# Attention weights laid out on the host, and the first transfers cut in panels

## The chip, the cores and the metric

The kernel runs on one NeuronCore of a Trainium2 chip. The metric is the device time of one execution in microseconds (us). A core has five engines with queues of their own, which are kept in step by semaphores only: TensorE (PE, with its weight loads as PEld), VectorE (DVE), ScalarE (ACT), GpSimd (POOL) and SyncE (SP), which here issues transfers only. ACT issues a few transfers too. SBUF is the working memory with 128 partitions, PSUM holds eight banks that matmuls write. `ps` is PSUM in the profile's names.

## What is computed

Four residual layers over x (8 sequences of 256 tokens, 128 features): attention A with a table of relative biases, a routed feed-forward net of 8 experts, causal attention B with a low-rank key/value, and the same feed-forward net again.

```python
x = L0_attn_a_x                                        # (8, 256, 128)
x = x + attn_a(layernorm(x), w_qkv, w_out, rel_bias)
x = x + ffn(layernorm(x), Wr, br, ln_g, ln_b, W1, b1, W2, b2)
x = x + attn_b(layernorm(x), w_kv_down, w_kv_up, w_q, w_out)
x = x + ffn(layernorm(x), ...)

def attn_a(x, w_qkv, w_out, rel_bias):                 # 16 heads of 64
    qkv = (x @ w_qkv.T).reshape(b, t, 64, 3, 16).transpose(3, 0, 4, 1, 2)
    q, k, v = qkv                                      # w_qkv: (3072, 128)
    scores = q @ k.T / 8 + rel_bias[j - i + t - 1]
    out = softmax(scores) @ v
    return merge_heads(out) @ w_out.T                  # w_out: (128, 1024)
```

Attention B has the weights `w_q` (128 x 1024), `w_kv_down` (128 x 128), `w_kv_up` (128 x 2048) and `w_out_b` (1024 x 128).

## The kernel before

The work is written out by hand in steps. A step `s` from 0 to 63 is one unit, `u`: two heads of one sequence, so there are `NU` = 64 units in an attention, eight to a sequence. Steps beyond 63 are the 25 tiles of the feed-forward net; then the same steps run again with `st` = 1 for attention B and the second net. Each engine runs its own list of these steps in order, so the order on an engine is that of its functions `begin` and `step`.

A unit goes this way. PE computes queries and keys of the unit into bank `PT_` (`QK(u)`, six matmuls of 256 columns in two groups of three: every product is split in a high and a low part, and `three` adds high*high, low*high and high*low). ACT copies them to `qk` (`T(u)`); only then may PE write `PT_` again. PE computes the scores (`S(u)`, 16 matmuls), for two units in a row on odd steps. DVE subtracts them from the bias table `T` and takes the minimum (`S(u)`, L1365). ACT takes the exponentials (L1046), DVE the reciprocal of their sums (L1378), POOL multiplies (L429), PE transposes (`TR`), DVE and ACT copy a half each from PSUM (`pt`, L1393 and L1034), PE multiplies by the values (`PV`, L742).

The high and low parts of the weights are made on the core. ACT writes the high part (`act_high`, L971) with a conversion to the narrower type, DVE the low part, the rest (`low`, L1232 and L1234). For attention A the weights come in as they are stored, with the features of x along the row, so the contraction is not on the partitions: `wqn`, `wkn`, `wvn` and `won` are loaded, PE transposes them into PSUM (`pe_weights`, `value_weights`, `extra`), and ACT and DVE read them from there. `w_part` n = 0 and 1 are queries and keys of units 0 to 3, n = 2 and 3 of units 4 to 7, n odd the keys.

The start, before step 0 ends, runs like this. SP issues in this order the first 128 KB of x (`x[:, 0:2]`), four transfers of halves of `wqn` and `wkn`, a half of `wvn`, the bias table for units 0 and 1 (`T[0:4]`, 512 KB), more of x, `T[4:8]`, `won`, `T[8:16]` and the rest of x. ACT issues the other halves (64 partitions each) of the same weights. DVE takes the statistics of x (`pre_a`), POOL the power, DVE normalises (`pre_a2`, tile `xh`), PE transposes (`pre_b`), ACT and DVE split it in `xth` and `xtl`. DVE then makes the low parts of panels 0 to 2, the bias table of units 0 and 1 (`biases(0)`, L1344 and L1345) and both low parts of the value weights, before its `S(0)`. POOL makes the tables of the other units.

The weights of attention B come during the first feed-forward net, on SP, once the 64th unit is done (L1785 to L1795): twelve transfers with rows of 64 or 128 elements for the order by unit. Behind them in SP's queue stand `results`, which write tiles of the net back.

Of the kernel before, what the change touches and what calls it, by code (L numbers as in the profile page):

```python
# [179 lines left out]
def build(nc, t):  # L180
# [148 lines left out]
    wq3 = t["w_qkv"].rearrange("(d c f h k) x -> c h d f k x", c=3, f=4, h=2, k=2)  # L329

    def heads(j, hh, a, b):

        return wq3[j, hh, :, a:b, :, :]

    def of_heads(w, a):

        return w[:, a:a + 1024].rearrange("p (f h k d) -> p h f k d", f=4, h=2, k=2)
# [268 lines left out]
    def pe_steps(st):  # L606
# [206 lines left out]
        def extra(s):  # L813
            for g in range(2 if s == 4 else 0):
                if g == 0:
                    pe.wait_ge(d_won, 16)
# [1039 lines left out]
```

## Time and profile before

| | us |
|---|---|
| median of 3 runs | 650.25 (649.43 to 650.32) |
| the profiled execution | 648.84 |
| its span, first to last instruction | 647.6 |
| PE busy | 625.2 (97%) |
| DVE busy | 511.1 (79%) |
| ACT busy | 524.6 (81%) |
| POOL busy | 354.9 (55%) |

The profile is of one execution. 1.2 us of its time lie outside the span. The busy time of PE contains the modelled ends of pipelined matmuls, so it is read beside the idle times in front of instructions. The chain of waits, followed back from the last instruction, tells what set the end.

### The profile page before, as it was taken

How to read it: one execution, taken by the hardware profiler on the slowest of the kernel's cores; microseconds unless marked ns; L12 is line 12 of the kernel's file. 1: busy time of each engine (PE TensorE's matmuls, PEld its weight loads, DVE VectorE, ACT ScalarE, POOL GpSimd, SP SyncE). 2: the span in 40 equal slices, each digit the busy share in tenths (PEclk: the TensorE clock that was granted, in tenths of full speed). 3: DMA queues.
4: the chain of work that ended last, by engine and by line, in shares of the span. 5: the costliest groups of instructions: out<-in, count | busy, mean ns of one | idle time of the engine just before them, and what ended most of it. 6: DMA issues, size and time to landing. Idle time of an engine off the chain costs nothing.

```text
span 647.6 us, 22119 instructions
## 1 busy us (share of the span) xinstructions
PE 625.2 (97%) x7454; PEld 537.3 (83%) x7454; DVE 511.1 (79%) x2211; ACT 524.6 (81%) x1776; POOL 354.9 (55%) x674
## 2 busy tenths in 40 slices
PE   5999999999999999999999899999999999999997
PEld 4678787877878788879988789888888988888997
DVE  4986878778887888888865787887988799898833
ACT  3898888889788878785675998998989898986664
POOL 5653645455475557643206554555757665772746
PEclk9999999999999999999999999999999999999999
DMA  8999989999991000133531100000000000113140
GB/s 263 317 307 308 289 211 319 313 310 311 282 287 41 3 2 27 43 100 83 166 107 37 40 3 3 8 2 6 7 7 21 16 4 2 36 49 93 55 129 18
DMA packets 90319, 74.78 MB, mean 115 GB/s; under 512 B 12225, under 2 KB 87111, under 8 KB 90080
## 3 DMA queue, kind: packets, MB, share of 16 engines
q1 hardware_dynamic: 86512, 66.24, 36.6%
q0 software_dynamic: 2848, 6.33, 3.0%
q8 instruction: 62, 1.02, 0.6%
q10 hardware_dynamic: 848, 0.79, 0.4%
q14 instruction: 49, 0.40, 0.2%
HBM read 19.93 MB, written 54.00 MB: 114 GB/s over the span
## 4 chain that ended last, share of the span: by engine, by line
PE 79%; DVE 7%; issue 4%; POOL 3%; ACT 3%; DMA 3%; SPq 1%; DVEq 0%; POOLq 0%; ACTq 0%
PE ps L578 16%; PE ps L694 13%; PE ps L742 13%; PE ps L573 10%; PE ps L575 8%; PE ps L574 8%; PE ps L848 5%; PE ps L864 4%; DVE ring L1365 2%; ACT ring L1046 2%; DMA T<-in_bias 1%; POOL out L449 1%; POOL ring L429 1%; PE ps L780 1%; DVE v L1330 1%
## 5 line engine op out<-in xcount | busy, mean ns | idle before, releaser
L429 POOL TENSOR_SCALAR ring<-ring,rs 128x256 f32<-128x256 f32 (+1 forms) x500 | 217.1, 451 | 129.4 <-DVE rs L1378 127.5
L1046 ACT ACTIVATE ring<-ring,mn 128x256 f32<-128x256 f32 (+1 forms) x512 | 243.7, 483 | 1.5 <-DVE mn L1365 1.4
L578 PE MATMUL ps<-ident,ring 128*128 128x128 f32 x896 | 122.0, 275 | 3.6 <-DVE ol L1337 1.8
L578 PEld LDWEIGHTS ps<-ident,ring 128*128 128x128 f32 x896 | 101.9, 142 | 12.5 <-issue 4.1
L694 PE MATMUL ps<-qk 64*64 64x256 f32 (+3 forms) x2048 | 107.1, 344 | 1.3 <-ACT qk L1018 0.8
L742 PE MATMUL ps<-pt,v 64*64 64x256 f32 (+3 forms) x2048 | 102.9, 338 | 2.0 <-ACT pt L1034 1.5
L1046 ACT ACTIVATION_READ_ACCUMULATOR ring<-ring,mn 128x1 f32 x512 | 101.7, 199 | 0.0
L742 PEld LDWEIGHTS ps<-pt,v 64*64 64x64 f32 x2048 | 76.5, 133 | 26.1 <-ACT pt L1034 6.6
L1393 DVE COPY pt<-ps 128x512 f32<-128x512 f32 (+1 forms) x128 | 75.5, 589 | 20.3 <-PE ps L578 18.8
L694 PEld LDWEIGHTS ps<-qk 64*64 64x64 f32 x2048 | 65.0, 133 | 28.4 <-issue 12.3
L1018 ACT COPY qk<-ps 128x512 f32<-128x512 f32 x128 | 74.3, 580 | 12.4 <-PE ps L575 12.2
L1365 DVE CUSTOM_DVE_ANT_0 ring<-ps,cm 128x128 f32<-128x128 f32 (+1 forms) x256 | 73.5, 352 | 0.9 <-PE ps L694 0.3
L1034 ACT COPY pt<-ps 128x512 f32<-128x512 f32 (+1 forms) x128 | 64.2, 502 | 2.0 <-PE ps L578 1.6
L1012 ACT ACTIVATE oh<-ps 128x256 fp32r<-128x256 f32 x128 | 41.9, 380 | 29.4 <-PE ps L742 29.1
L573 PE MATMUL ps<-xth,wqkh 128*128 128x256 f32 x192 | 65.2, 339 | 0.0
L1095 ACT ACTIVATE f_ht<-ps,f_w 128x128 f32<-128x128 f32 x136 | 38.4, 377 | 22.6 <-PE ps L848 22.6
L1365 DVE CUSTOM_DVE_ANT_0 ring<-ps,T 128x256 f32<-128x256 f32 x136 | 55.9, 420 | 0.0
L1365 DVE CUSTOM_DVE_ANT_1 ring<-ps,T 128x256 f32<-128x256 f32 x120 | 50.3, 419 | 5.4 <-PE ps L694 4.5
L574 PE MATMUL ps<-xth,wqkl 128*128 128x256 f32 x192 | 54.2, 282 | 0.0
L575 PE MATMUL ps<-xtl,wqkh 128*128 128x256 f32 x192 | 54.2, 282 | 0.0
L1330 DVE COPY v<-ps 64x512 f32<-64x512 f32 x64 | 44.0, 688 | 12.9 <-PE ps L575 11.0
L864 PE MATMUL ps<-w,f_ht 128*128 (+1 forms) x400 | 52.4, 277 | 0.5 <-ACT f_ht L1095 0.4
(210 smaller groups left out, 1297.3 us busy)
## 6 DMA issues: line engine op xcount, KB each, us to landing
xs_scratch<-f_ys SPq DMA_DIRECT2D x16, 2064.0 KB, 21.5
yr_scratch<-f_ys SPq DMA_DIRECT2D x8, 1024.0 KB
f_xs<-xs_scratch SPq DMA_DIRECT2D x50, 129.0 KB, 2.3
w<-in_W SPq DMA_DIRECT2D x16, 256.0 KB, 6.0
xs_scratch<-f_ys SPq DMA_DIRECT2D x2, 1677.0 KB, 20.5
yr_scratch<-f_ys SPq DMA_DIRECT2D x25, 64.0 KB, 1.8
T<-in_bias SPq DMA_DIRECT2D x2, 512.0 KB, 8.2
T<-in_bias SPq DMA_DIRECT2D x1, 1024.0 KB, 10.7
```

Of the source, the lines that this page charges most:

```text
L429: i = pool.tensor_scalar(part, part, rs[:, q], 1.0, ALU.mult, ALU.mult)
L573: pe.matmul(out, ah, bh, start=first, stop=False)
L574: pe.matmul(out, al, bh, start=False, stop=False)
L575: return pe.matmul(out, ah, bl, start=False, stop=last)
L578: return pe.transpose(out, src, ident if order is None else order)
L694: i = pe.matmul(PS[u % 2][hh][cols, 256 * it:256 * it + w], qk[rows, 64 * n:64 * n + 64], qk[rows, 256:256 + w], start=True, stop=True)
L742: i = pe.matmul(PO[hh][64 * k:64 * k + 64, lo:256], a_v[b % 2][rows, q, 64 * (c + k):64 * (c + k) + 64], a_pt[(U0 + u + k) % 2][rows, half ...
L864: i = pe.matmul(y_bank(n)[:, 0:128], f_ht[n % 3][:, 128 * f:128 * f + 128], w2[:, bass.ds(e * 4 + f, 1), :].rearrange("p a n -> p (a n)"), ...
L1018: act.copy(a_qk[(U0 + u) % 2][:, :], PT_[:, :]).then_inc(a_t, 1)
L1046: i = act.activation(part, part, ACT.Exp, bias=mn[:, q], scale=-1.0, accum_out=sm[:, q])
L1365: i = dve.tensor_tensor_reduce(scores(ring, hh, it, w), by_64(bank[:, 256 * it:256 * it + w]), table(st, head_of(c, hh), it), 1.0, BIG, AL ...
L1393: dve.tensor_copy(pt[:, 1, r], PP[1][:, r]).then_inc(v_pt1, 1)
```

## The change

1. The host (numpy) lays out `w_qkv`, `w_out_a`, `w_q`, `w_kv_up` and `w_out_b` so that the contraction is on the partitions and the columns stand in the order of the units.
2. No weight is transposed on PE. `pe_weights`, `value_weights` and `extra` are gone from PE; ACT and DVE read the raw weights in SBUF and wait for the transfer instead of for PE. `wvh` and `wvl` are written in halves of 512 contiguous columns.
3. Queries and keys come in three panels instead of two: units 0 and 1, 2 and 3, 4 to 7. So there are six parts (`products(0)` to `products(5)`), four of 256 columns and two of 512.
4. Transfers at the start: ACT issues panel 0, panel 2 and the two halves of the value weights, over all 128 partitions; SP issues x, panel 1, then the table. The third table transfer is cut in two, with `won` between.
5. ACT runs parts 0 to 3 before `xth`, parts 4 and 5 after it and before `T(0)`, and the two halves of the value weights on steps 1 and 2 instead of both on step 1. DVE runs parts 0 and 1 between the statistics and the normalisation, 2 and 3 behind it, the second value half and parts 4 and 5 on step 2.
6. For attention B four transfers stand where twelve stood.

```diff
+PANELS = [(0, 2), (2, 4), (4, 8)]
...
+    raws = at_first(pre, *(sb(n, [128, 1024], scope=pre) for n in ("wqkn0", "wvn0", "wqkn1", "wvn1")))
...
             if b == 0:
-                pe.wait_ge(a_wv, 3 if st else 2)
-                pe.wait_ge(v_wv, 3 if st else 2)
+                pe.wait_ge(a_wv, 3 if st else half_ + 1)
+                pe.wait_ge(v_wv, 3 if st else half_ + 1)
...
-            if st == 0 and u in (0, 4):
-                pe.wait_ge(a_m, 2 + u // 2)
-                pe.wait_ge(v_m, 2 + u // 2)
+            for g, (first, _) in enumerate(PANELS):
+                if st == 0 and u == first:
+                    pe.wait_ge(a_m, 2 * g + 2)
+                    pe.wait_ge(v_m, 2 * g + 2)
...
             pre_b(0)
-            for n in range(4):
-                if n % 2 == 0:
-                    pe.wait_ge(d_wqk[n // 2], 64)
-                pe_weights(n)
...
         def products(*ns):
             for n in ns:
-                act.wait_ge(t_m, n + 1)
-                act_high(w_part(wqkh, n), m_bank(n)[:, :], a_m, scale=w_scale(n))
+                act.wait_ge(d_wqk[n // 2], 16)
+                act_high(w_part(wqkh, n), w_raw(n), a_m, scale=w_scale(n))
...
     def act_program():
+        for g in (0, 2):
+            act.dma_start(raw(g), t["w_qkv"][:, panel(g)]).then_inc(d_wqk[g], 16)
         for g in range(2):
-            for j, w in enumerate((wqn, wkn)):
-                act.dma_start(w[64:128, 4 * g:4 * g + 4, :], heads(j, 1, 2 * g, 2 * g + 2)).then_inc(d_wqk[g], 16)
-        act.dma_start(wvn[64:128, :, :], heads(2, 1, 0, 4)).then_inc(d_wv, 16)
+            act.dma_start(wvn[g][:, 0:512], t["w_qkv"][:, 2048 + 512 * g:2560 + 512 * g]).then_inc(d_wv[g], 16)
...
     def sp_program():
         sp.dma_start(x[:, 0:2, :], xv[:, 0:2, :]).then_inc(d_x[0], 16)
-        for g in range(2):
-            for j, w in enumerate((wqn, wkn)):
-                sp.dma_start(w[0:64, 4 * g:4 * g + 4, :], heads(j, 0, 2 * g, 2 * g + 2)).then_inc(d_wqk[g], 16)
-        sp.dma_start(wvn[0:64, :, :], heads(2, 0, 0, 4)).then_inc(d_wv, 16)
+        sp.dma_start(raw(1), t["w_qkv"][:, panel(1)]).then_inc(d_wqk[1], 16)
         sp.dma_start(a_T[:, 0:4, :], t["bias"][:, 0:4, :]).then_inc(d_T[0], 16)
         sp.dma_start(x[:, 2:4, :], xv[:, 2:4, :]).then_inc(d_x[1], 16)
         sp.dma_start(a_T[:, 4:8, :], t["bias"][:, 4:8, :]).then_inc(d_T[1], 16)
-        sp.dma_start(won[:, :], t["w_out_a"]).then_inc(d_won, 16)
-        sp.dma_start(a_T[:, 8:16, :], t["bias"][:, 8:16, :]).then_inc(d_T[2], 16)
+        sp.dma_start(a_T[:, 8:12, :], t["bias"][:, 8:12, :]).then_inc(d_T[2], 16)
+        sp.dma_start(won[:, :, :], t["w_out_a"]).then_inc(d_won, 16)
+        sp.dma_start(a_T[:, 12:16, :], t["bias"][:, 12:16, :]).then_inc(d_T[3], 16)
...
+        sp.dma_start(bq[:, :], t["w_q"]).then_inc(d_bq, 16)
+        sp.dma_start(bu[:, :], t["w_kv_up"]).then_inc(d_bu, 16)
         sp.dma_start(bkd, t["w_kv_down"]).then_inc(d_bkd, 16)
-        sp.dma_start(bo[:, :, :], t["w_out_b"].rearrange("(c p) n -> p c n", p=128)).then_inc(d_bo, 16)
+        sp.dma_start(bo[:, :, :], t["w_out_b"]).then_inc(d_bo, 16)
```

The order on DVE from the normalisation to the first scores. `wqkl` and `wvl` are low parts of weights, `cT` and `T` the bias table, `ISA ring,mn` is the first operation of `S(0)`. Before:

```order
L1252 TENSOR_SCALAR xh<-row,mv,rstd 128x128 [waits p_pow0]
L1252 TENSOR_SCALAR xh<-row,mv,rstd 128x128
L1232 TENSOR_TENSOR xtl<-ps,xth 128x256 [waits a_x]
L1234 SCALAR_TENSOR_TENSOR wqkl<-ps,wqkh 128x512 [waits a_m]
L1232 TENSOR_TENSOR wqkl<-ps,wqkh 128x512 [waits a_m]
L1234 SCALAR_TENSOR_TENSOR wqkl<-ps,wqkh 128x512 [waits a_m]
L1294 COPY run<-rows_e 128x8 [waits p_set]
L1344 COPY cT<-T 128x4 [waits d_T0,v_c]
L1345 TENSOR_TENSOR T<-cT,T 128x1024 [waits v_c]
L1232 TENSOR_TENSOR wvl<-ps,wvh 128x4x2x64 [waits a_wv,v_c]
L1232 TENSOR_TENSOR wvl<-ps,wvh 128x4x2x64 [waits a_wv]
L1365 ISA ring,mn<-ps,T 128x4x64 [waits t_s,p_set]
```

And of the change, on the same engine and at the same place:

```order
L1202 SCALAR_TENSOR_TENSOR wqkl<-wqkn,wqkh 128x256 [waits a_m]
L1200 TENSOR_TENSOR wqkl<-wqkn,wqkh 128x256 [waits a_m]
L1220 TENSOR_SCALAR xh<-row,mv,rstd 128x128 [waits p_pow0]
L1220 TENSOR_SCALAR xh<-row,mv,rstd 128x128
L1202 SCALAR_TENSOR_TENSOR wqkl<-wqkn,wqkh 128x256 [waits a_m]
L1200 TENSOR_TENSOR wqkl<-wqkn,wqkh 128x256 [waits a_m]
L1200 TENSOR_TENSOR xtl<-ps,xth 128x256 [waits a_x]
L1262 COPY run<-rows_e 128x8 [waits p_set]
L1312 COPY cT<-T 128x4 [waits d_T0,v_c]
L1313 TENSOR_TENSOR T<-cT,T 128x1024 [waits v_c]
L1200 TENSOR_TENSOR wvl<-wvn,wvh 128x512 [waits a_wv,v_c]
L1337 ISA ring,mn<-ps,T 128x4x64 [waits t_s,p_set]
```

Two low parts of 256 columns now stand ahead of the normalisation and two behind it; of the value weights one half is left ahead of `S(0)`.

DVE between the last operation of `S(1)` and `S(2)`. `COPY v` takes values from PSUM, `stats` to `rstd` are the statistics of sequence 1. Before:

```order
L1330 COPY v<-ps 64x512 [waits t_v]
L1232 TENSOR_TENSOR wqkl<-ps,wqkh 128x512 [waits a_m]
L1239 BN_STATS stats<-row 128x6 [waits d_x1]
L1242 BN_STATS stats<-row 128x6
L1243 BN_AGGR mv<-stats 128x2 [waits v_c]
L1244 BN_AGGR mv<-stats 128x2
L1248 TENSOR_SCALAR rstd<-mv 128x2 [waits v_c]
L1330 COPY v<-ps 64x512 [waits t_v]
L1378 RECIPROCAL rs<-sm 128x4 [waits a_ex]
```

And of the change:

```order
L1200 TENSOR_TENSOR wvl<-wvn,wvh 128x512 [waits a_wv]
L1202 SCALAR_TENSOR_TENSOR wqkl<-wqkn,wqkh 128x512 [waits a_m]
L1200 TENSOR_TENSOR wqkl<-wqkn,wqkh 128x512 [waits a_m]
L1298 COPY v<-ps 64x512 [waits t_v]
L1207 BN_STATS stats<-row 128x6 [waits d_x1]
L1210 BN_STATS stats<-row 128x6
L1211 BN_AGGR mv<-stats 128x2 [waits v_c]
L1212 BN_AGGR mv<-stats 128x2
L1216 TENSOR_SCALAR rstd<-mv 128x2 [waits v_c]
L1298 COPY v<-ps 64x512 [waits t_v]
L1350 RECIPROCAL rs<-sm 128x4 [waits a_ex]
```

Three operations of 512 columns stand where one stood.

The start of ACT's queue, up to `T(1)`, with the transfers that it issues. Before:

```order
L1209 DMA wqn<-in_w_qkv 64x2x256 [waits barrier_Pool_Activation_PE_DVE_SP_release]
L1209 DMA wkn<-in_w_qkv 64x2x256
L1209 DMA wqn<-in_w_qkv 64x2x256
L1209 DMA wkn<-in_w_qkv 64x2x256
L1210 DMA wvn<-in_w_qkv 64x4x256
L971 ACT_TABLE_LOAD
L971 ACTIVATE xth<-ps 128x256 [waits t_x]
L971 ACTIVATE wqkh<-ps 128x512 [waits t_m] x3
L1018 COPY qk<-ps 128x512 [waits t_t]
L971 ACTIVATE wvh<-ps 128x4x2x64 [waits t_wv] x2
L1018 COPY qk<-ps 128x512 [waits t_t]
```

And of the change:

```order
L1176 DMA wqkn<-in_w_qkv 128x512 [waits barrier_Pool_Activation_PE_DVE_SP_release]
L1176 DMA wqkn<-in_w_qkv 128x1024
L1178 DMA wvn<-in_w_qkv 128x512 x2
L930 ACT_TABLE_LOAD
L930 ACTIVATE wqkh<-wqkn 128x256 [waits d_wqk0] x2
L930 ACTIVATE wqkh<-wqkn 128x256 [waits d_wqk1] x2
L930 ACTIVATE xth<-ps 128x256 [waits t_x]
L930 ACTIVATE wqkh<-wqkn 128x512 [waits d_wqk2] x2
L989 COPY qk<-ps 128x512 [waits t_t]
L930 ACTIVATE wvh<-wvn 128x512 [waits d_wv0]
L989 COPY qk<-ps 128x512 [waits t_t]
```

Each group of weights now waits for its own transfer, and the two parts of panel 2 stand between `xth` and the first `COPY qk`, which is `T(0)`.

## Rows read from the trace of the kernel before

**Rows 1.** The page: the span, and the chain that ended last, by engine.

```profile
span 647.6 us, 22119 instructions
...
PE 79%; DVE 7%; issue 4%; POOL 3%; ACT 3%; DMA 3%; SPq 1%; DVEq 0%; POOLq 0%; ACTq 0%
```

**Rows 2.** Stretches: busy us of PE, PEld, DVE, ACT, POOL; granted clock; DMA share; GB/s.

```profile
8.00:9.00 1.00, 0.34 (x2) 0.00 (x0) 0.69 (x1) 0.72 (x2) 0.71 (x5) 1.00 1.13 232
...
14.00:15.00 1.00, 1.00 (x18) 0.63 (x21) 0.96 (x3) 0.94 (x3) 0.50 (x2) 1.00 1.07 438
...
60.00:290.00 230.00, 228.42 (x2736) 185.26 (x2734) 190.04 (x793) 193.58 (x630) 127.62 (x244) 1.00 0.66 183
```

**Rows 3.** The chain that ended last, 0 to 60 us: start, us, what.

```profile
4.71 7.90 DMA T<-in_bias
...
15.44 0.42 DVE ring L1365
...
27.67 0.61 DVE pt L1393
28.32 0.66 PE ps L578 x4
```

**Rows 4.** Timeline of PE: start, us, operation, count, idle before and its releaser.

```profile
9.22 1.11 PE L578 MATMUL ps<-ident,wqn 128*128 128x128 f32 x4 [0.87 <-DMA wkn<-in_w_qkv]
...
10.84 0.56 PE L573 MATMUL ps<-xth,wqkh 128*128 128x256 f32 x1
...
11.84 0.41 PE L574 MATMUL ps<-xth,wqkl 128*128 128x256 f32 x1
12.05 0.41 PE L575 MATMUL ps<-xtl,wqkh 128*128 128x256 f32 x1
12.26 1.26 PE L578 MATMUL ps<-ident,wvn 128*128 128x128 f32 x8
...
14.16 1.96 PE L694 MATMUL ps<-qk 64*64 64x256 f32 x32
...
16.27 0.28 PE L574 MATMUL ps<-xth,wqkl 128*128 128x256 f32 x1
16.39 0.28 PE L575 MATMUL ps<-xtl,wqkh 128*128 128x256 f32 x1
```

**Rows 5.** Timeline of DVE, 3 to 28 us.

```profile
3.35 0.29 DVE L1239 BATCH_NORM_STATS2 stats<-row 128x6 f32<-128x128 f32 x1 [3.35 <-DMA row<-in_x]
...
5.23 0.60 DVE L1252 TENSOR_SCALAR xh<-row,mv,rstd 128x128 f32<-128x128 f32 x2 [0.91 <-POOL rstd L395]
7.09 0.42 DVE L1232 TENSOR_TENSOR xtl<-ps,xth 128x256 fp32r<-128x256 f32 x1 [1.26 <-ACT xth L971]
...
14.17 1.29 DVE L1232 TENSOR_TENSOR wvl<-ps,wvh 128x512 fp32r<-128x512 f32 x2
...
19.04 0.69 DVE L1232 TENSOR_TENSOR wqkl<-ps,wqkh 128x512 fp32r<-128x512 f32 x1
19.64 0.28 DVE L1239 BATCH_NORM_STATS2 stats<-row 128x6 f32<-128x128 f32 x1
```

**Rows 6.** Timeline of ACT, 4 to 13 us.

```profile
4.35 1.28 ACT L971 ACT_TABLE_LOAD   x1 [4.35 <-issue]
6.67 0.38 ACT L971 ACTIVATE xth<-ps 128x256 fp32r<-128x256 f32 x1 [1.04 <-PE ps L578]
...
12.50 0.58 ACT L1018 COPY qk<-ps 128x512 f32<-128x512 f32 x1 [1.54 <-PE ps L575]
```

**Rows 7.** ACT's queue: start and us of the last transfer that it issues.

```profile
3.69 0.63 ACTq L1210 DMA_DIRECT2D wvn<-in_w_qkv  x1
```

**Rows 8.** SP's queue near 300 us, and a low part made from SBUF (tile `bq`).

```profile
299.96 2.90 SPq L1789 DMA_DIRECT2D bq<-in_w_q  x4
...
308.06 3.48 SPq L1753 DMA_DIRECT2D yr_scratch<-f_ys  x5
...
L1234 DVE SCALAR_TENSOR_TENSOR wqkl<-bq,wqkh x1: 1215/1215/1215, 323.3 to 323.3; 128x1024 fp32r<-128x1024 f32 x1
```

More of the change, by code:

```diff
@@ L328, in build, with panel, raw @@
     xv = t["x"].rearrange("b (s p) d -> p (b s) d", p=128)
[L329 to L337, printed above, removed]
+    def panel(g):
+        a, b = PANELS[g]
+        return slice(256 * a, 256 * b)
+    def raw(g):
+        a, b = PANELS[g]
+        return wqkn[a // 4][:, 256 * (a % 4):256 * (a % 4) + 256 * (b - a)]
     def load(engine, values, a, b, most):
@@ L811, in post_d @@
             pe.matmul(PX[:, n8:2 * n8], ones[:, :], h, start=True, stop=True).then_inc(t_cnt, 1)
[L813 to L816, printed above, removed]
-                bank = spare(("wo", g), v_wo, g + 1)
-                for j in range(4):
-                    i = tr(bank[:, 128 * j:128 * j + 128], won[:, 512 * g + 128 * j:512 * g + 128 * j + 128])
-                i.then_inc(t_wo, 1)
         def XT(g):
@@ L1125, in begin, with value_weights @@
         def begin():
+            products(0, 1, 2, 3)
             pre_b(0)
-            products(0, 1, 2)
-        def value_weights():
-            for g in range(2):
-                act.wait_ge(t_wv, g + 1)
-                act_high(by_parity(wvh[:, :])[:, 4 * g:4 * g + 4], by_unit(ps[4 + g][:, :]), a_wv)
+            products(4, 5)
+        def value_weights(g):
+            act.wait_ge(d_wv[g], 16)
+            act_high(halves(wvh, g), wvn[g][:, 0:512], a_wv)
         def step(s):
@@ L1352, in S @@
                 dve.wait_ge(p_set, k_T0)
+            if st == 0 and u in (1, 3):
+                dve.wait_ge(v_wv, (u + 1) // 2)
+            if st == 0 and u == 2:
+                dve.wait_ge(v_m, 2 * len(PANELS))
             if st == 0 and u in (2, 4, 6):
@@ L1571, in begin, with value_weights @@
             pre_a(0)
+            products(0, 1)
             pre_a2(0)
+            products(2, 3)
             pre_b(0)
-            products(0, 1, 2)
-        def value_weights():
-            for g in range(2):
-                low(by_parity(wvl[:, :])[:, 4 * g:4 * g + 4], by_unit(ps[4 + g][:, :]),
-                    by_parity(wvh[:, :])[:, 4 * g:4 * g + 4], a_wv, g + 1, v_wv)
+        def value_weights(g):
+            low(halves(wvl, g), wvn[g][:, 0:512], halves(wvh, g), a_wv, g + 1, v_wv)
         def step(s):
@@ L1586, in step @@
                 start_rows()
-            if st == 0 and s == 1:
-                value_weights()
+            if st == 0 and s in (1, 2):
+                value_weights(s - 1)
+            if st == 0 and s == 2:
+                products(4, 5)
             if s % 2 == 0 and 6 <= s < NU:
@@ L1831, with _by_units, _by_halves, _w_qkv @@
           "L0_ffn_ln_b": "ln_b", "L0_ffn_W1": "W1", "L0_ffn_b1": "b1", "L0_ffn_W2": "W2", "L0_ffn_b2": "b2"}
+def _by_units(a):
+    return a.reshape(128, 4, 2, 2, 64).transpose(0, 1, 3, 2, 4).reshape(128, 1024)
+def _by_halves(a):
+    return a.reshape(128, 4, 2, 2, 64).transpose(0, 2, 1, 3, 4).reshape(128, 1024)
+def _w_qkv(a):
+    q, k, v = a.reshape(64, 3, 1024 // 64, 128).transpose(1, 3, 2, 0).reshape(3, 128, 1024)
+    q, k = _by_units(q), _by_units(k)
+    panels = [w[:, 128 * a:128 * b] for a, b in PANELS for w in (q, k)]
+    return np.concatenate(panels + [_by_halves(v)], axis=1)
+_LAYOUT = {"w_qkv": _w_qkv,
+           "w_out_a": lambda a: a.reshape(128, 8, 128).transpose(2, 1, 0),
+           "w_q": _by_units,
+           "w_kv_up": lambda a: np.concatenate([_by_units(a[:, :1024]), _by_halves(a[:, 1024:])], axis=1),
+           "w_out_b": lambda a: a.reshape(8, 128, 128).transpose(1, 0, 2)}
 def kernel(**inputs):
```

90 lines of the change are left out of this document (33 added, 57 removed).

## The prediction

> **What bounds the kernel now.** I read the page first: a span of 647.6 us, of which PE holds 79% of the chain that ended last [rows 1]. In the table of stretches PE is busy for 228.42 of the 230 us from 60 to 290 [rows 2]. There a saving on any other engine is worth nothing, and the change takes no work from PE there. So the whole question is how early PE enters that steady flow. The chain read in order of time answers it [rows 3]: SP's issues, then the wait for the first bias table, which lands at 4.71 + 7.90 = 12.61 us, then DVE without a break (table, low parts of the value weights, S(0) at 15.44 and so on) to its copy `pt` at 27.67, and from 28.32 on PE. The reader is to see that the PE transposes of the weights are not on this path. What counts is the time at which DVE ends that `pt` copy. It ends at 27.67 + 0.61 = 28.28; I call that the hand-over. A gain there is carried through a PE-bound kernel to the end, one for one.
>
> **From S(0) to the hand-over, DVE's work grows.** DVE runs from 15.44 to 28.28 without idle time worth naming, 12.84 us. In this stretch the change drops one low part of 512 columns and adds three: the second half of the value weights and both parts of panel 2. One costs 0.60 us from PSUM (19.04 to the next start at 19.64 [rows 5]) and, from SBUF, 1215 ns for 1024 columns, so 0.61 for 512 [rows 8]. Net +1.22 us, giving 14.06. I take it in full, since DVE has no gap there to hide it. The bounds are 0 (if DVE would have waited at the next scores anyway) and 1.22. So the hand-over is S(0) + 14.06, and S(0) must start before 14.22 for a gain.
>
> **When S(0) can start.** Before, DVE reached it at 15.44, right behind the two `wvl` (14.17 + 1.29) [rows 5], while PE had begun S(0) at 14.16 [rows 4], 1.3 us ahead. The table was late, and the scores were nearly as late. I work out both chains of the change.
>
> *The table.* The transfers of both issuing engines share the engines that move them, so I count bytes, and take it that the two queues get equal shares. SP has 128 KB of x, 256 of panel 1 and 512 of table: 896 KB, and as much again goes to ACT's queue meanwhile, 1792 KB or 1835 thousand bytes. The first 128 KB of x were used at 3.35 [rows 5]; the rest is 1704 thousand bytes. The stretch from 8 to 9 us, with weight rows of 1 KB, moved 232 GB/s; that from 14 to 15, with table rows of 4 KB, 438 [rows 2]. The change has rows of 2 to 4 KB. So 7.3 or 3.9 us more: 10.7 or 7.2, and I take 9.0. Either beats 12.61. By the Trainium skill, "DMA: Bandwidth & Descriptors", section "Bandwidth", a 1 MB load runs at 341 GB/s; as an estimate that would put the table at 8.3. `cT`, table and low part of the first value half cost some 1.4 + 0.6 us, so DVE is free by 11.7 even where it waits for ACT's `wvh`. The table is no longer what holds S(0).
>
> *The scores.* (a) ACT's last issue began at 3.69 as the fifth [rows 7]; the change has four, so it is over near 3.6, and the 1.28 us table load [rows 6] ends near 4.9. (b) Panel 0 lands between 4.2 and 5.0 by the same byte count, so ACT makes part 0 at 4.9 to 5.3 (0.38 for 256 columns [rows 6]) and part 1 by 5.5. (c) DVE makes both low parts by 6.0 (0.42 each, overlapping). Before, the normalisation started at 5.23 [rows 5]; now it stands behind them and starts at 5.95: this is 0.7 us lost. (d) From the normalisation to the start of `xtl` took 7.09 - 5.23 = 1.86, so `xtl` is at 7.8 and done at 8.2; parts 2 and 3 fit into DVE's wait. Panel 1 (between 4.8 and 6.1) is in time for them. (e) QK(0) starts at 8.3 instead of 10.84 [rows 4]. From its first matmul to `T(0)` took 12.50 - 10.84 = 1.66 [rows 4, 6]. That puts `T(0)` at 9.95. (f) In front of `T(0)` ACT now waits for panel 2, behind 768 KB of its queue: 1442 thousand bytes after 3.35 take 3.3 to 6.2 us, landing 6.6 to 9.5. Two parts, each at the 0.58 that ACT takes for 512 columns [rows 6], then end at 7.8 to 10.7; I take 9.1, hidden by QK(0), and keep 0.7 us late as the bound. (g) `T(0)` ends at 10.55, QK(1) starts at 10.7. Before, the value transposes filled this place, 12.26 to 13.3 [rows 4]. (h) QK(1) takes 1.3 at 0.21 a matmul, to 12.0. (i) S(0) is half of 32 matmuls that took 1.89 to the next start, so 0.95; at half the rate 1.7 to 1.9.
>
> **The clock of PE.** The granted clock reads 1.00 in the stretches I show [rows 2], but the rows of PE say otherwise: 256 columns step by 0.21 us up to 12.05, which is the level of 1.2 GHz, and by 0.12 at 16.27, that of 2.4 GHz [rows 4]. It rose after PE had worked without a break from 9.22. In the change PE has a gap between QK(0) and QK(1), so it may rise later than 12. The Trainium skill, "TensorE: Matmul & The Clock Gate", "Part 1: The HAM clock gate (the "warmup" mystery)", says that the clock depends on how busy PE has recently been; by that rule the removal of the transposes, which kept PE busy, speaks against this change, and the later trace agrees in so far as the rate rose only after unbroken work; by it alone the time would be that of rival B. The prices are from rows: fast from 12.0, S(0) is done at 12.95 and starts on DVE at 13.0; rising inside S(0), 13.3; slow throughout, 13.75, and S(1) is then another 0.3 late for DVE.
>
> **The sum.** Hand-over at 13.3 + 14.06 = 27.36 against 28.28: 0.9 us earlier. Span 646.7, time 648.84 - 0.9 = 647.9 for an execution like the profiled one. This one lies 1.4 us below the median of 650.25, so I subtract the same 0.9 there: 649.35. ACT is nearly as full as DVE before the hand-over, but it loses one 512 part and is released by PE's `T(2)` even earlier than DVE; I cost it at nothing, and if that cover is gone it costs up to the 0.6 of one part. POOL's tables wait for landings only: the second comes before 14.3 and is needed with S(2) after 20; nothing.
>
> **The parts worth nothing.** The 32 transposes on PE (8 in 1.26 us [rows 4]) lie before the hand-over, where PE is not the bound. The eight of `won` also go, with the wait of the next `xh` transpose for `wo`; DVE sets that stretch, so nothing. The split of the third table transfer: the table of the last units is asked for after 20 us; nothing. Near 300 us SP issues twelve transfers from 299.96 and reaches its first result at 308.06 [rows 8]. Eight issues fewer are about 5 us for SP, but PE and its neighbours go on meanwhile, and `bq` is first split by DVE at 323.3 [rows 8]: hidden by the tiles, nothing. If a result tile were awaited it would be a gain, bounded by 5 us; no row shows such a wait.
>
> **Rivals.** *A, the lead is carried in full:* PE is at the fast level by 12, or DVE's added 1.22 us fall into waits. Hand-over 1.3 to 2.4 us early: 648.4. For it: the first value half and the table leave DVE idle before S(0). Against: rows 5 have no gap behind S(0). *B, nothing is left:* the clock rises late (13.75 + 14.06 + 0.3 = 28.1), or panel 2 lands at 9.5: 650.1, the gain all spent on DVE's added parts and PE's slow start. *C, slower:* ACT's queue gets much less than half of the bandwidth, since x, panel 1, both tables and `won` follow on SP without pause. `T(0)` stands behind panel 2; S(0) on DVE then passes 14.22 when the panel lands after about 9.7, and it is slower by over 1.3 us when it lands after 11.1. At 12 us: 652.5. Against: 786 thousand bytes from 3.35 to 12 would be 91 GB/s, below half of 232, the slower rate shown. *D, the change doesn't do what it says:* some later wait, such as PE's for the added values at step 3, takes the lead away; 650.25, part of B's chance.
>
> **How the numbers follow.** A measurement of this kernel can tell 0.2%, 1.3 us, from no change. The forecast (0.3 to 1.3 us faster) has 0.48, A 0.31, B with D 0.16, C 0.05. Predicted: 649.35. The range reaches over A and B to 647.9 and 650.6, leaving C and the far ends. Faster by over 0.2% has A's chance and a little of the forecast's edge, 0.33; slower has C and a crumb, 0.06; the rest, 0.61, is within 0.2%.
>
> **What would show it.** Right, step by step: the first table lands before 11; QK(0) starts near 8.3; `T(0)` is near 10 with no wait for panel 2; DVE waits for PE, not for a transfer, at S(0), near 13.3; three low parts stand between S(1) and S(2); DVE's `pt` copy ends near 27.4; the stretch from 60 to 290 us keeps 228 us of PE. Wrong: a chain that still holds a transfer after 10 us, S(0) after 14, or a difference that arises only after 60 us.

## The result, and the profile after

The change makes the kernel slower: 655.09 us median (654.20 to 655.45, 4 runs) against 650.23 before, a ratio of 1.0080 with a 95% interval of 1.0063 to 1.0097. The profiled execution took 654.2 us. Its page begins with the span, 5.2 us over that of before [rows 1]:

```profile
span 652.8 us, 22049 instructions
```

Two readings say where to search. The stretch from 60 to 290 us has not moved (228.42 us of PE before [rows 2]). And the fourth pair of scores behind the hand-over, the same work in both kernels, starts 5.21 us later. The table of stretches of after (columns as in rows 2), and the rows of PE's timeline, first of before and then of after:

```profile
60.00:290.00 230.00, 229.25 (x2736) 186.48 (x2729) 190.12 (x793) 193.95 (x630) 129.64 (x249) 1.00 0.60 174
```

```profile
52.02 1.96 PE L694 MATMUL ps<-qk 64*64 64x256 f32 x32
```

```profile
57.23 1.96 PE L677 MATMUL ps<-qk 64*64 64x256 f32 x32
```

So the whole loss lies ahead of 57 us. From here on I compare kernels at this pair of scores: whatever follows it takes 595.6 us in both profiles. The chain of after up to there, beside [rows 3]:

```profile
0.81 3.65 DMA row<-in_x
...
12.99 1.96 PE ps L677 x16
15.09 0.42 DVE ring L1337
...
17.93 1.90 DVE wvl L1200
...
28.28 2.99 DVE wo L1200 x2
31.27 0.61 DVE pt L1365
31.93 1.01 PE ps L570 x4
32.94 3.16 PE ps L677 x32
```

The table of biases has left the chain, as forecast, and S(0) starts on DVE at 15.09, even 0.35 before its old time. The loss comes behind it. The hand-over has moved from 28.28 to 31.88, and PE's first work behind it is slow. Two rows are far too long. DVE's timeline of after (beside [rows 5]):

```profile
4.48 0.29 DVE L1207 BATCH_NORM_STATS2 stats<-row 128x6 f32<-128x128 f32 x1 [4.48 <-DMA row<-in_x]
...
11.92 0.69 DVE L1200 TENSOR_TENSOR wvl<-wvn,wvh 128x512 fp32r<-128x512 f32 x1 [1.55 <-ACT wvh L930]
17.85 1.98 DVE L1200 TENSOR_TENSOR wvl<-wvn,wvh 128x512 fp32r<-128x512 f32 x1
...
28.28 2.99 DVE L1200 TENSOR_TENSOR wo<-won,wo 128x512 fp32r<-128x512 f32 x2
31.19 0.68 DVE L1365 COPY pt<-ps 128x512 f32<-128x512 f32 x1
```

The same operation on the same shape takes 0.69 us at 11.92 and 1.98 at 17.85; two of them take 2.99 at 28.28, where before they took 1.29. Beside both long rows POOL works on a bias table. POOL's timeline of after, and then the two rows of before in which the low part, with PSUM as its source, ran beside the same POOL operation without loss:

```profile
17.39 1.89 POOL L451 TENSOR_TENSOR T<-cT,T 128x1024 f32<-128x1024 f32 x1
...
28.43 2.29 POOL L451 TENSOR_TENSOR T<-cT,T 128x1024 f32<-128x1024 f32 x1
```

```profile
26.38 1.29 DVE L1232 TENSOR_TENSOR wo<-ps,wo 128x512 fp32r<-128x512 f32 x2
```

```profile
26.53 1.89 POOL L459 TENSOR_TENSOR T<-cT,T 128x1024 f32<-128x1024 f32 x1
```

The times fit an exclusion that lasts for a whole instruction. POOL's table operation ends at 17.39 + 1.89 = 19.28; `wvl` ends 0.55 later, at 19.83, about the 0.6 that one part takes. In the second case DVE comes first: one part runs from 28.28 to about 28.9, POOL waits for it (2.29 instead of 1.89, until 30.72), and the second part ends at 31.27.

Then the clock. PE's timeline of after [rows 4], and its stretches:

```profile
24.18 0.50 PE L565 MATMUL ps<-wvh,xth 128*128 128x512 f32 x1 [2.08 <-DVE mn L1337]
...
31.93 1.01 PE L570 MATMUL ps<-ident,ring 128*128 128x128 f32 x4 [2.24 <-DVE pt L1365]
32.87 3.23 PE L677 MATMUL ps<-qk 64*64 64x256 f32 x32
```

```profile
30.00:32.00 2.00, 0.07 (x1) 0.07 (x2) 2.00 (x3) 2.00 (x8) 0.72 (x1) 1.00 1.10 334
32.00:34.00 2.00, 2.00 (x16) 1.31 (x20) 0.98 (x3) 1.31 (x6) 0.15 (x1) 0.52 1.10 331
34.00:36.00 2.00, 2.00 (x28) 1.13 (x28) 0.98 (x5) 0.00 (x0) 1.69 (x4) 0.63 1.10 334
```

PE stood idle for 2.24 us, then worked at the level of 1.2 GHz until about 35.5 (a granted clock of 0.52 from 32 to 34, and 1.00 again behind 35.5). The transposes took 1.01 instead of 0.66 and the scores 3.23 instead of 1.96: 1.6 us. Together, 3.6 for the hand-over and 1.6 for the clock are the 5.2. The clock of after had been low once before, behind the gap of 2.08 us: from about 25.4 to 28.7, where eight transposes took 1.91 us instead of 1.04. That cost nothing here: DVE, which sets the hand-over, did not wait for PE in that time, and PE then waited 2.24 us for DVE.

### The profile page after: what moved, and what is told of

It is laid out like the page before. It is cut to its first block, busy times and chain, and to the rows that moved or that the text cites. A ratio compares the mean times of both kernels' runs of the same rounds, so it can differ in the third digit from the quotient of the medians.

```text
span 652.8 us, 22049 instructions
## 1 busy us (share of the span) xinstructions
PE 624.7 (96%) x7422; PEld 535.3 (82%) x7422; DVE 514.0 (79%) x2213; ACT 525.2 (80%) x1778; POOL 356.4 (55%) x674
## 4 chain that ended last, share of the span: by engine, by line
PE 80%; DVE 7%; issue 4%; ACT 3%; POOL 3%; DMA 2%; DVEq 0%; SPq 0%; POOLq 0%; ACTq 0%
PE ps L570 16%; PE ps L677 14%; PE ps L725 13%; PE ps L565 10%; PE ps L566 8%; PE ps L567 8%; PE ps L822 5%; PE ps L838 5%; DVE ring L1337 2%; ACT ring L1017 2%; POOL ring L422 1%; PE ps L763 1%; DVE v L1298 1%; PE ps L781 1%; DVE pt L1365 1%
## 5 line engine op out<-in xcount | busy, mean ns | idle before, releaser
L677 PE MATMUL ps<-qk 64*64 64x256 f32 (+3 forms) x2048 | 109.4, 349 | 1.3 <-ACT qk L989 0.8
L989 ACT COPY qk<-ps 128x512 f32<-128x512 f32 x128 | 74.3, 580 | 14.4 <-PE ps L567 14.3
```

Source lines behind the costliest of these rows:

```text
L677: i = pe.matmul(PS[u % 2][hh][cols, 256 * it:256 * it + w], qk[rows, 64 * n:64 * n + 64], qk[rows, 256:256 + w], start=True, stop=True)
L989: act.copy(a_qk[(U0 + u) % 2][:, :], PT_[:, :]).then_inc(a_t, 1)
```

## The experiments

The theory (E in the expectations) is that a DVE operation with two inputs in SBUF and a POOL operation that reads SBUF exclude each other, and that the change put its low parts (two inputs in SBUF now, one in PSUM before) beside POOL's table operations. The first rival (S) is that the loss comes from the start, where x lands at 4.48 instead of 3.35 and S(0) runs at 1.2 GHz. The second point, C, is that PE's gap lowers its clock. Every kernel is read by its ratio to the kernel before on the same chip and by three times of its profile: the end of DVE's `pt` copy, the duration of the scores behind it, and the start of the fourth pair.

| kernel | ratio (95%) | `pt` ends | scores | fourth pair |
|---|---|---|---|---|
| before | 1 | 28.26 | 1.96 | 52.02 |
| after | 1.0080 (1.0063 to 1.0097) | 31.87 | 3.23 | 57.23 |
| won_alone | 1.0055 (1.0038 to 1.0073) | 30.60 | 3.62 | 56.01 |
| won_psum | 1.0047 (1.0031 to 1.0062) | 30.31 | 1.96 | 54.05 |
| pool_quarters | 1.0055 (1.0036 to 1.0075) | 31.03 | 3.60 | 56.41 |
| pe_busy | 1.0063 (1.0040 to 1.0086) | 31.98 | 1.96 | 55.74 |
| pool_writes | 1.0029 (1.0016 to 1.0043) | 28.87 | 3.61 | 54.29 |
| x_split | 1.0064 (1.0043 to 1.0085) | 31.06 | 3.69 | 57.59 |
| lows_early | 1.0011 (1.0001 to 1.0021) | 27.60 | 2.13 | 51.61 |
| tables_2 | 1.0056 (1.0039 to 1.0073) | 32.09 | 1.96 | 55.82 |
| lows_tab4 | 1.0056 (1.0037 to 1.0074) | 30.51 | 3.55 | 55.92 |
| wo_late | 1.0017 (1.0006 to 1.0027) | 27.11 | 2 x 1.09 | 52.39 |
| wo_late_x | 1.0006 (0.9991 to 1.0021) | 27.40 | 2 x 1.09 | 52.67 |
| wo_apart | 1.0005 (0.9995 to 1.0016) | 27.39 | 2 x 1.09 | 52.03 |

In the rows from after to x_split, and in tables_2 and lows_tab4, the last column follows, within 0.1 us, from the two ahead of it and from what else ran at the lower clock (the transposes, 0.35 in after and 0.45 in x_split, where `ps<-pt,v` adds 0.64). For won_alone, 30.60 - 28.26 = 2.34 and 3.62 - 1.96 = 1.66 make 4.00; the pair is 3.99 late. For pool_writes 0.61 + 1.65 = 2.26, and 2.27 is measured.

**One part of the change alone: won_alone.** The kernel before, with only `won` laid out by numpy and split from SBUF.

```diff
-    won, = at_first(pre, sb("won", [128, 1024], scope=pre))
+    won, = at_first(pre, sb("won", [128, 8, 128], scope=pre))
...
-                bank = spare(("wo", g), v_wo, g + 1)
-                for j in range(4):
-                    i = tr(bank[:, 128 * j:128 * j + 128], won[:, 512 * g + 128 * j:512 * g + 128 * j + 128])
...
-                low(wo[:, 4 * g:4 * g + 4, 128:256], ps[bank_of[("wo", g)]][:, :].rearrange("p (c n) -> p c n", c=4),
+                low(wo[:, 4 * g:4 * g + 4, 128:256], won[:, 4 * g:4 * g + 4, :],
```

> The kernel before with one part of the change: the output weights come laid out by the host and are split straight from SBUF, without the eight PE transposes; all else as before. Theory E (exclusion: a DVE operation with two SBUF inputs and a POOL operation that reads SBUF do not run at the same time): the two low parts of wo fall on POOL's table operation of 1.9 us and take some 3.0 us together instead of 1.29, the copy of pt ends 1.7 us later than at 28.28, and PE has a gap behind which its clock may fall for another 1.6 us: 1.7 to 3.3 us slower. Rival S (the loss of the change comes from the late x and the slow clock of PE at the start, not from SBUF inputs): no difference, within 0.5 us, and the low parts keep 1.3 us.

DVE's, POOL's and PE's timelines of won_alone:

```profile
27.01 2.99 DVE L1222 TENSOR_TENSOR wo<-won,wo 128x512 fp32r<-128x512 f32 x2
```

```profile
27.17 2.28 POOL L459 TENSOR_TENSOR T<-cT,T 128x1024 f32<-128x1024 f32 x1
```

```profile
30.65 0.66 PE L578 MATMUL ps<-ident,ring 128*128 128x128 f32 x4 [2.39 <-DVE pt L1383]
31.24 3.62 PE L694 MATMUL ps<-qk 64*64 64x256 f32 x32
```

The part that I had called worth nothing costs 3.5 us by itself, a little more than the 1.7 to 3.3 expected, though x, the tables and all other weights come as in the kernel before. S can't explain that. Of the 2.34 us at `pt`, 1.70 are the `wo` row; 0.63 stand already at S(0), which began at 16.06 here behind a wait for PE: PE's rate rose at about 14.4 in this profile and between 12.3 and 13.3 in that of before, and PE began S(0) at 14.78 instead of 14.16. Nothing of `won` has run by then, so this share is not the edit's work on DVE; why the rate rose later is open.

**The same part undone: won_psum.** The changed kernel, with `won` through PE and PSUM again (the diff above the other way round).

> The changed kernel with this one part undone: the output weights go through PE and PSUM again. Theory E: the low parts of wo take 1.3 us again, so the copy of pt ends 1.7 us earlier than at 31.87, and PE's gap before it shrinks from 2.24 to about 0.5 us; if the clock then stays up, another 1.6 us. 1.7 to 3.3 us faster than the change: 651.8 to 653.4. Rival S: no faster than the change, 655.

DVE's timeline of won_psum:

```profile
28.43 1.29 DVE L1213 TENSOR_TENSOR wo<-ps,wo 128x512 fp32r<-128x512 f32 x2
```

The two `wo` parts are back at 1.29 us beside POOL's 1.89, the gap in front of the last transposes falls to 0.32 and the scores are fast. The pair of scores gains 3.2 us. The median gains only 1.5, and at 653.63 lies just above the range expected. Two things show why. Behind the pair the profiles of the experiments have 0.5 to 4 us more (the span less the pair's start is 597.8 here, 595.6 in before and after, 599.5 at most). In won_psum nearly all of it is idle time of PE around the two feed-forward nets: in the 20 us that begin 280 us behind the pair PE is busy for 17.71 (18.64 in before), and in those that begin 520 us behind it for 16.86 (17.87). Why PE waits longer there is open. And the ten runs of won_psum differ in their clock: four with a mean granted clock of 1.000 took 651.93 to 653.23, three with 0.995 took 654.84 to 654.86, so the clock fell in some runs and not in others. So mechanisms are read from the pair, and what a version is worth from the ratio.

**The other engine: pool_writes.** DVE's program stays as it is, POOL no longer reads. The bias of units 2 to 7 is left out, so only the time to the pair is comparable.

```diff
-            pool.tensor_tensor(v, over_keys(e), v, ALU.subtract).then_inc(p_T, 1)
+            pool.memset(v, 0.0).then_inc(p_T, 1)
```

> The changed kernel with POOL's three table operations (T = cT - T, 128 x 1024, two inputs in SBUF) replaced by a memset of the same tile to zero: the bias of units 2 to 7 is left out, so values and routing behind it differ, and only the time to 60 us is comparable. DVE's code and order are untouched. E (it is POOL's reading of SBUF that shuts DVE's two-input operations out): wvl(1) falls from 1.98 to 0.69 us and wo's two parts from 2.99 to 1.29, hand-over 31.88 - 1.3 - 1.7 = 28.9, PE's gap under 0.5 us, the scores behind it at 1.96 us, and the scores pair that stood at 57.23 near 52.6. If any POOL access to the same tile is enough, the durations stay near 2 and 3 us for as long as the memsets overlap them. S: hand-over and scores pair as in the changed kernel.

DVE's, POOL's and PE's timelines of pool_writes:

```profile
17.84 0.69 DVE L1200 TENSOR_TENSOR wvl<-wvn,wvh 128x512 fp32r<-128x512 f32 x1
...
26.98 1.29 DVE L1200 TENSOR_TENSOR wo<-won,wo 128x512 fp32r<-128x512 f32 x2
```

```profile
27.11 0.95 POOL L451 MEMSET T<- 128x1024 f32 x1
```

```profile
27.19 0.63 PE L570 MATMUL ps<-ident,ring 128*128 128x128 f32 x4 [0.84 <-ACT pt L1005]
28.93 0.65 PE L570 MATMUL ps<-ident,ring 128*128 128x128 f32 x4 [1.12 <-DVE pt L1365]
29.52 3.61 PE L677 MATMUL ps<-qk 64*64 64x256 f32 x32
```

Both rows fall to the price that I had used, and the hand-over is at 28.87, where E put it at 28.9. The memset lies inside `wo`'s time and costs it nothing (it is also the shorter operation, 0.95 us, but all of it overlaps `wo`): a POOL operation that only writes doesn't exclude DVE, one that reads does. The size of the clock was missed. PE had gaps of 0.84 and 1.12 us and its clock fell all the same, so the pair is at 54.29, not 52.6.

**Is it the whole instruction: pool_quarters.** POOL's table operation in four, of 256 columns each.

```diff
-            pool.tensor_tensor(v, over_keys(e), v, ALU.subtract).then_inc(p_T, 1)
+            for i in range(4):
...
+                k_ = pool.tensor_tensor(v[:, i:i + 1, :], e1, v[:, i:i + 1, :], ALU.subtract)
+            k_.then_inc(p_T, 1)
```

> The changed kernel with POOL's table operation of 1024 columns cut in four of 256, no other edit. Theory E, held for a whole instruction: a DVE operation waits for one quarter at most, 0.5 us, so the low part that took 1.98 us takes 0.7 to 1.2 and the two of wo take 1.4 to 2.3 instead of 2.99; hand-over 1.3 to 2.4 us earlier and perhaps 1.6 from the clock: 651.2 to 653.8. If the way were shared by turns within an instruction, or if the long low parts had another cause (rival S), nothing changes: 655, and the low parts stay at 2.0 and 3.0 us.

DVE's and POOL's timelines of pool_quarters:

```profile
20.37 1.10 DVE L1203 TENSOR_TENSOR wqkl<-wqkn,wqkh 128x512 fp32r<-128x512 f32 x1
...
28.72 1.71 DVE L1203 TENSOR_TENSOR wo<-won,wo 128x512 fp32r<-128x512 f32 x2
```

```profile
18.26 3.68 POOL L453 TENSOR_TENSOR T<-cT,T 128x256 f32<-128x256 f32 x4
...
28.88 3.16 POOL L453 TENSOR_TENSOR T<-cT,T 128x256 f32<-128x256 f32 x4
```

DVE now waits for one quarter at a time (`wvl` takes 0.85), and POOL for DVE between its quarters (3.68 us for four, 2.33 where DVE leaves it alone). `wo` drops by 1.28 us, while the two panel parts rise to 1.10 each. So a wait has the length of one instruction of the other engine. Shorter ones only share out what must pass: `pt` ends 0.84 us earlier, the median of 654.00 lies above the 651.2 to 653.8 expected, and its ratio can't be told from that of the change with certainty.

**The clock: pe_busy.** The changed kernel, with 18 transposes of the identity into an unused bank in PE's gap.

```diff
+                if U0 + u == 1 and jt:
+                    for _ in range(18):
+                        pe.transpose(ps[6][:, 0:128], ident, ident)
```

> The changed kernel with 18 transposes of the identity on PE (into a bank that is overwritten later, result unused) in the gap of 2.24 us in front of the second half of TR(1). Theory C (PE's clock falls to 1.2 GHz because of that gap): the stretch of 3.4 us at half clock that began near 31.8 is gone, the scores of units 4 and 5 take 1.9 us instead of 3.2, and the time is 1.3 to 1.6 us shorter, 653.6. Rival (the clock falls for another reason, the first gap or the power of the start): the stretch stays, no difference. Work added in a gap costs nothing itself while it ends before the copy of pt at 31.87.

PE's timeline of pe_busy:

```profile
32.62 1.96 PE L677 MATMUL ps<-qk 64*64 64x256 f32 x32
```

DVE's collision stays (`wo` 2.99 us, `pt` ends at 31.98), the largest gap left just ahead of the scores is 0.95 us, and they run in 1.96. The pair gains 1.5 us of the 5.2; the medians, 654.32 and 655.09, don't settle it by themselves. One profile would not either: the fall near 25.4 us is missing from it too, behind a gap of 1.55 us that holds no added work (2.08 in after). But the mean granted clock of the runs goes the same way: 0.994 to 0.997 in all four of the change, 1.000, 1.000, 0.999 and 0.997 in pe_busy.

**The start: x_split.** The first 128 KB of x in two queues.

```diff
+        act.dma_start(x[:, 1:2, :], xv[:, 1:2, :]).then_inc(d_xb, 16)
...
-        sp.dma_start(x[:, 0:2, :], xv[:, 0:2, :]).then_inc(d_x[0], 16)
+        sp.dma_start(x[:, 0:1, :], xv[:, 0:1, :]).then_inc(d_x[0], 16)
```

> The changed kernel with its first 128 KB of x asked for in two halves, the second by ACT's queue ahead of panel 0. Everything else stays, the excluded operations too. S: x is then used at 3.4 to 3.8 instead of 4.48, S(0) and the hand-over move by as much, and 0.7 to 1.1 us come off the time, more if the clock of PE rises earlier with it. E: the start may move, but the waits beside POOL's table operations hang on the tables and on steps, so at most the same 0.7 to 1.1 us; wvl(1) and wo still take 2 and 3 us. If x lands no earlier in two queues: no difference.

DVE's timeline of x_split:

```profile
2.94 0.29 DVE L1209 BATCH_NORM_STATS2 stats<-row 128x6 f32<-128x128 f32 x1 [2.94 <-DMA row<-in_x]
...
5.98 0.42 DVE L1204 SCALAR_TENSOR_TENSOR wqkl<-wqkn,wqkh 128x256 fp32r<-128x256 f32 x1 [2.07 <-ACT wqkh L931]
```

x comes 1.54 us earlier, and panel 0 pays: its first low part, behind which the normalisation stands, moves from 5.36 to 5.98. S(0) is at 15.42 and gains nothing: x and panel 0 share what the start can move. One thing had been expected otherwise: `wvl` takes 0.69 us here, not 2. POOL's set-up is done earlier, its table operation ends at 15.92 + 1.89 = 17.81, and `wvl` starts at 18.33, so they no longer meet. That is why `pt` ends 0.81 us ahead of the change. It is lost again behind it, where PE waited 2.82 us and the clock stayed low for the transposes, the scores (3.69) and the products with the values. Why x is late in the change at all was not tried by itself, so the cause is not shown. The queues' rows fit: ACT's transfers are all asked for by 2.7 us, where before they went out until 4.3, so more is under way beside x.

**The low parts moved away: lows_early, tables_2, lows_tab4.** lows_early has two edits. The value and panel 2 low parts stand ahead of S(0), in time in which DVE was idle, and POOL's last table operation stands in step 2 instead of 4, away from `wo`. The two other kernels have one edit each.

```diff
-BIASES = {1: 2, 2: 4, 4: 6}
+BIASES = {1: (2,), 2: (4, 6)}
...
-            if st == 0 and s in (1, 2):
-                value_weights(s - 1)
-            if st == 0 and s == 2:
-                products(4, 5)
+            if st == 0 and s == 1:
+                value_weights(0)
+                value_weights(1)
...
+                products(4, 5)
```

> The changed kernel with the two value low parts and both low parts of panel 2 made by DVE ahead of S(0), in time in which it was idle (8.5 to 11.9 us and before 15.1), and POOL's last table operation moved from step 4 to step 2. The low part of won stays at step 4. E (a DVE operation with two inputs in SBUF and a POOL operation that reads SBUF exclude each other): the parts are off the stretch from S(0) on, so 3 x 0.61 us of work and the 1.3 us of wait beside POOL's table go. won's low part no longer meets a table operation and takes 1.3 us instead of 2.99. Hand-over 31.88 - 1.8 - 1.3 - 1.7 = about 27.1 and no slow clock behind it (1.6 us): 5 to 6 us off the changed kernel's time, 649.5 to 650.5. S (the loss is the late start and the slow clock at the start): the parts only stand elsewhere, S(0) on DVE is later by their 2.4 us if anything, and the time stays at 654 or above.

Nearly the whole loss is gone; what is left (0.01 to 0.21%) is at the edge of what can be told. DVE's timeline and the chain of lows_early:

```profile
14.21 0.69 DVE L1201 TENSOR_TENSOR wvl<-wvn,wvh 128x512 fp32r<-128x512 f32 x1 [1.44 <-ACT wvh L931]
...
25.49 1.51 DVE L1201 TENSOR_TENSOR wo<-won,wo 128x512 fp32r<-128x512 f32 x2
```

```profile
22.57 4.71 POOL ring L422 x8
27.32 1.09 PE ps L571 x8
```

The value part takes 0.69 us and `wo` meets only POOL's short `ring` operations (0.46 each). The exclusion now costs POOL more than DVE: its eight `ring` operations take 4.71 us here and 3.71 in wo_late, where no `wo` stands beside them. PE now waits for POOL, not for DVE.

> The changed kernel with one edit: POOL's last table operation in step 2, behind the one that stands there, instead of step 4. E: the low part of won meets no table operation and takes 1.3 to 1.5 us instead of 2.99; the hand-over is 1.5 us earlier and PE's gap ahead of it falls from 2.24 to under 1, so that its clock does not fall (another 1.3 to 1.6 us). In step 2 the two table operations stand together for 3.8 us beside three low parts, which may cost them up to another 1.9 us there. So 651.5 to 653.5, against 655.1. S: no effect, 654 or above.

> The changed kernel with the value and panel 2 low parts ahead of S(0), and POOL's last table operation left in step 4 (the other half of lows_early). E: the low part of won meets the table again and takes 2.99 us; hand-over near 29, PE's gap about 2 us with the slow clock behind it; 651.5 to 653.5. Together with the run tables_2 it divides the 4.8 us that lows_early gave. If it equals lows_early (650.3), it was not the exclusion at won's low part that counts, but only the work ahead of it.

Alone the edits give 1.4 and 1.3 us at the pair, together 5.6, and E's numbers missed the table's share. In tables_2 the conflict has only changed its place. The last table operation leaves `wo` (1.29 us again) and meets the low parts of step 2. DVE's and POOL's timelines of tables_2:

```profile
20.57 2.38 DVE L1201 TENSOR_TENSOR wqkl<-wqkn,wqkh 128x512 fp32r<-128x512 f32 x1
```

```profile
20.17 2.23 POOL L451 TENSOR_TENSOR T<-cT,T 128x1024 f32<-128x1024 f32 x1
```

So `pt` ends at 32.09, no earlier than in the change, and what it gains is the clock (1.96 us for the scores). In lows_tab4 the parts ahead of `wo` are free of POOL, `pt` ends 1.36 us earlier, but `wo` takes 2.99 us, PE has gaps of 1.66 and 1.78 us, and the slow scores stay at 3.55. Only with both does no part meet a table operation. All three kernels start like the change (x at 4.5 to 4.7, S(0) on DVE not ahead of 15.1), and with that same start lows_early has lost nearly the whole loss, so S falls as its cause.

**A better version: wo_late, wo_late_x, wo_apart.** In wo_late the low part of `won` also leaves the stretch, to step 9 behind the hand-over; wo_late_x adds x_split; wo_apart keeps POOL's last table in step 4, since nothing is left there to collide with, and gives the parts to steps 9 and 11.

```diff
-            for g in range(2 if s == 4 else 0):
+            for g in {9: (0,), 11: (1,)}.get(s, ()):
```

> The kernel lows_early with the low part of won moved from step 4 to step 9, behind the hand-over, where PE has work queued; won lies in other memory, so that nothing waits for it. E: 1.3 us of DVE leave the stretch ahead of the hand-over: about 26.0, 648.5 to 649.5, a little below the kernel before. If the part is not hidden at step 9, it costs PE what it gave, and the time equals that of lows_early. S: 654, as above.

> wo_late and x_split together. E: hand-over 0.7 to 1 us ahead of that of wo_late, 647.5 to 648.7, faster than the kernel before by 0.2 to 0.4%. If S(0) is set by the parts that now stand ahead of it on DVE, and not by x, the two kernels are equal.

> wo_late with POOL's last table operation left in step 4, and the two parts of won in steps 9 and 11, one each, on ACT and DVE. No DVE operation with two inputs in SBUF is left from S(0) to the hand-over. E: POOL reaches its eight ring operations 1.9 us earlier than in wo_late, where they ended last ahead of PE, and ACT's 1.16 us for both high parts no longer delay PE by about 1 us in step 9. Hand-over near 26; 648.5 to 649.5, faster than the kernel before by 0.1 to 0.3%. If ACT, without a gap in this stretch, sets the hand-over: 650, as before.

All three miss: DVE is free early, but the time equals that of before, or lies a little above it (wo_late, 0.06 to 0.27%). Only the alternative named for wo_apart, that ACT sets the hand-over, came true. PE's timeline of wo_apart says who comes last now:

```profile
26.80 1.31 PE L570 MATMUL ps<-ident,ring 128*128 128x128 f32 x8 [0.48 <-ACT pt L1003]
28.04 1.09 PE L677 MATMUL ps<-qk 64*64 64x256 f32 x16
29.44 1.09 PE L677 MATMUL ps<-qk 64*64 64x256 f32 x16 [0.31 <-issue]
```

DVE's `pt` ends at 27.39, and PE's two idle times are not DVE's. The first is a wait for ACT, which is busy for 5.98 of the 6 us from 20 to 26 and sets this point now (in wo_late it is still POOL, whose `ring` operations end the wait of 0.91 us ahead of PE's transposes at 25.14). In step 9 the high parts of `won` on ACT then hold PE up again: in wo_late PE waits 0.77 us for ACT's `pt` there, and the pair is at 52.39. In wo_late_x the earlier x is lost on the known conflict, met in a new place: `wvl` (14.79, 1.80 us) runs into POOL's table operation (14.15 + 1.89 = 16.04), and S(0) starts at 16.51. No version beats the kernel before by what this measurement can tell (wo_apart: 0.9995 to 1.0016).

## Why the prediction was wrong

I forecast 649.35, a hand-over at 27.36 and 0.06 for slower; it is 655.09, with the hand-over at 31.88.

**The price of the added low parts.** This step failed, and it decides the case. I took 0.61 us per 512 columns from a row near 323 us [rows 8] and called its bounds 0 and 1.22. The price is right where POOL does not read: 0.69 at 11.92, 0.60 each for the panel parts at 19.83 and 20.43. But the row comes from a place where POOL is idle, while `wvl` and `wo` here stand beside POOL's tables. The one cost 1.29 more and the other 1.70, so the term "12.84 + 1.22" was too small at both ends.

**"The parts worth nothing": `won`.** I counted only what goes (eight transposes and a wait) and not that the low part changes its source from PSUM to SBUF. That costs 1.70 us on DVE and, by won_alone, 3.5 us with what follows: the largest term of all.

**"POOL's tables wait for landings only; nothing."** The landings did come earlier, but the tables of the change wait for something else: POOL's own set-up, which ends at 14.95 instead of 12.58, and the first table operation follows at once. The later x explains 1.13 us of that, and 1.08 are the same exclusion in the other direction. A set-up operation of POOL that reads SBUF stands beside DVE's own table operation, which the change moved from 12.91 to 9.14. POOL's timeline of before, and POOL's and DVE's of after:

```profile
7.87 0.26 POOL L524 CAST full_e<-f_k 128x96 f32<-128x96 int32 x1
```

```profile
9.15 1.34 POOL L516 CAST full_e<-f_k 128x96 f32<-128x96 int32 x1
```

```profile
9.14 1.22 DVE L1313 TENSOR_TENSOR T<-cT,T 128x1024 f32<-128x1024 f32 x1
```

Without these 1.08 us POOL's second table operation would end near 18.2 and cost `wvl` some 0.2 instead of 1.29, an estimate from these rows. And I had not set POOL's rows beside DVE's further on. Work of 16.79 us between S(0) and the hand-over, where I had 14.06, is the forecast plus 1.29 and 1.70, less 0.26 elsewhere in the stretch. The Trainium skill states the rule in "SBUF — State Buffer", section "SBUF: two separate sides": whichever of a DVE operation with two SBUF inputs and a GpSimd operation that reads SBUF starts first keeps the shared ports for its whole instruction, and the other waits until it has ended. The trace agrees in each point (1.98 and 2.99 us, 2.29 for POOL's own, 0.69 and 1.29 where POOL writes only). By it the sum would have been a hand-over near 30.4 and a forecast of slower; it is the rival that was missing.

**When S(0) can start.** The order of the steps was right and each is a little late. x is used at 4.48, not 3.35, and from there QK(0) is at 9.04 (8.3), T(0) at 10.70 (9.95), QK(1) at 11.34 (10.7), S(0) on PE at 12.92 (12.0). S(0) ran at 1.2 GHz, the dearest of my three cases, and its 16 matmuls took 2.0 us where I had at most 1.9, so DVE began at 15.09 instead of 13.3 (0.9 from the start, 0.9 from the clock); "S(0) after 14" was the sign I had named. With my own 14.06 behind it this makes a hand-over of 29.15, 0.9 later than before, or some 651.1: rival B and past it. C ended on the right side by the wrong cause. The table had landed when DVE came to it at 8.91, inside the range, and `T(0)` did not wait for panel 2.

**The clock.** I priced it only at the start. A lower clock behind a later wait, 1.6 us here, was in no rival: the step that a delay of the hand-over is carried "one for one" had left it out. Here the 3.6 us were carried one for one and then charged again.

**What held.** The table left the chain; PE's work from 60 to 290 stayed; the transfers near 300 us brought nothing; the first transposes of PE were not on the path.

The errors add up: S(0) 1.79 late, 2.73 more work than I counted and 1.6 of clock are 6.1 us, the 5.2 lost and the 0.9 that I had promised.

## What to carry to other kernels

A price is a row and its neighbours. Before an operation's input moves from PSUM to SBUF, look at what POOL does at that time, and take the price from a row that has the same company; and where POOL's work can stand elsewhere, move all the conflicts at once, since one moved alone may only meet the next. Ahead of an engine-bound stage a delay can cost more than itself, for PE may come back at half its clock.
